# A transformer layer on one core: where the first x is normalized, and who normalizes the first feed-forward rows

## The chip, the cores and the metric

One Trainium2 chip, one of its cores. The metric is the device time of one execution in microseconds. The kernel is written with one block of instructions per engine (TensorE, VectorE, ScalarE, GpSimd and SyncE, which issues all transfers), synchronized by semaphores; each engine works through its own list in order.

## The reference

16 batches of 512 rows of 512 numbers, 16 heads of 32, a feed-forward width of 2048:

```python
emb = silu(sin_emb(timestep)) @ W_ada + b_ada
scale, shift = split(emb, 2)
x = ln(src) * (1 + scale) + shift
q, k, v = x @ Wq + bq, x @ Wk + bk, x @ Wv + bv
scores = q @ k.T / sqrt(32) + attention_bias          # 16 x 16 x 512 x 512 biases, 268 MB
probs = softmax(where(mask, -inf, scores))
x = x + ((probs @ v) @ Wo + bo)
h = ln(x) * g2 + beta2
x = x + (gelu2(h @ W1 + b1) @ W2 + b2)                # gelu2(t) = t * sigmoid(1.702 t)
out = rotations of x's groups of four columns by theta and phi
```

## The kernel before

All large products are made of parts: each float32 operand is split into a high part (rounded by ScalarE) and a low part (operand minus high part, by VectorE or GpSimd), and three matmuls add up to one product.

**The setup block** (`setup_block`) runs first, as a block of its own, and a barrier of all engines ends it. SyncE loads small inputs, W_ada, the first batch's x (`load_x(sp, 0)`) and Wq, Wk, Wv in this order. VectorE makes the angles and silu, TensorE the modulation (`mod`), ScalarE scales Wq and makes the high parts WH of the three weights, VectorE their low parts WL.

**The attention stage** (`attention_stage`) goes over the batches in bodies: START prepares batch 0, then one body for each batch, with 64 slots in each body; x of the next batch is normalized and projected in the slots of the present one. Before slot 0 of START, VectorE takes the statistics of batch 0's x (`moments`, L874, and `aggregate`, L883) and GpSimd makes rstd (`spread_of`, L628 and L630) and the normalized rows (`norm`, L635). TensorE turns x (L716); ScalarE and VectorE modulate it and GpSimd makes its low part (`split_x`, L640). SyncE has in START's order: five bias loads (L546), three small loads and Wo (L574 to L576), the store of the normalized rows (`normal_rows`, L595, waits for `normed`), the load of the next x (L282, waits for that store and for the turning), the mask, and copies of q's and k's rows into the stacked form that the scores need (`stack_rows`, L560). VectorE's statistics of the next x stand among its low parts of q and k.

**The feed-forward stage** (`ffn_stage`) takes the batches in pairs p, each of q = p. For the first pair everything ahead of the eight pair steps is written out at the start of the stage: `project` (L1409) multiplies the context of row tile j by Wo, `modulate` (GpSimd, L1636) and `add` (VectorE, L1735 to L1744) make the residual row y and its mean and variance, `power` (GpSimd) makes rstd (L1645) and adds the second bias b2 (L1655), VectorE's `normalize` (L1751) makes z in place, `turn` (TensorE, L1421) turns z, `take_columns` and `split_columns` (ScalarE L1509 and L1520, VectorE L1789) make the parts of h. The row tiles are j = 0 to 7, four for each batch e of the pair. Then come eight steps s: seven products of the first layer (L1368, a Strassen-like scheme over the two batches), the gelu, and the second layer's matmuls onto ps_out (L1388). In the first pair only, each step also makes the parts of W1 for the step after it (`make_sums` on GpSimd, L1616 to L1621; `make_w1` on ScalarE L1494 and VectorE L1727) and of W2 (`make_w2`, ScalarE L1499, GpSimd L1625), stores them to DRAM for the later pairs, and in steps 4 to 7 GpSimd modulates the first batch's and second batch's rows of the next pair. In every step GpSimd makes two low parts of the gelu's output (`split_g`, L1607). SyncE's order in these steps is written out in `first`.

GpSimd's list in a step of the first pair is: make_sums(s + 1), modulations if any, split_g(2s), make_w2(2s), split_g(2s + 1), make_w2(2s + 1). TensorE takes the results in the step after.

## Time and profile before

| | us |
|---|---|
| three timed runs | 3285.91, 3292.41, 3293.02 (median 3292.41) |
| the profiled execution, its own time | 3286.79 |
| its span, first to last instruction | 3285.0 |
| TensorE busy | 3159.6 (96%) |
| VectorE, ScalarE, GpSimd busy | 2141.5, 1859.9, 2015.2 |
| mean granted TensorE clock | 0.993 |
| attention stage | about 34 to 1660 us of the span |
| feed-forward stage | about 1662 us to the end |

The profile is of one execution. The timeline shows each instruction with its start in microseconds of the span, its length, and in brackets how long its engine had idled before it and what ended that. The busy share of an engine says little of one stage; the waits in a stage do.

### The profile page before, as it was taken

How to read it: one execution, taken by the hardware profiler on the slowest of the kernel's cores; microseconds unless marked ns; L12 is line 12 of the kernel's file. 1: busy time of each engine (PE TensorE's matmuls, PEld its weight loads, DVE VectorE, ACT ScalarE, POOL GpSimd, SP SyncE). 2: the span in 40 equal slices, each digit the busy share in tenths (PEclk: the TensorE clock that was granted, in tenths of full speed). 3: DMA queues.
4: the chain of work that ended last, by engine and by line, in shares of the span. 5: the costliest groups of instructions: out<-in, count | busy, mean ns of one | idle time of the engine just before them, and what ended most of it. 6: DMA issues, size and time to landing. Idle time of an engine off the chain costs nothing. (4 is left out here: it accounts for less than half of the span.)

```text
span 3285.0 us, 52375 instructions
## 1 busy us (share of the span) xinstructions
PE 3159.6 (96%) x16592; PEld 2373.3 (72%) x16592; DVE 2141.5 (65%) x4445; ACT 1859.9 (57%) x4041; POOL 2015.2 (61%) x1247
## 2 busy tenths in 40 slices
PE   5999999999999999999969999999999999999998
PEld 4777777777777777767638688787877868687787
DVE  3777778777777777877757654554645555464542
ACT  2777777777777777777725243342434434253443
POOL 3888888888878888878745633435333443434413
PEclk9999999999999999999989999999999999999999
DMA  5999999998999999998857677675767757586665
GB/s 188 263 267 272 261 274 279 263 265 270 261 271 267 268 261 264 275 270 261 259 157 269 211 246 222 188 254 180 256 205 221 243 185 247 181 261 207 200 204 166
DMA packets 440432, 785.15 MB, mean 239 GB/s; under 512 B 57024, under 2 KB 106176, under 8 KB 440160
## 3 DMA queue, kind: packets, MB, share of 16 engines
q1 hardware_dynamic: 440160, 781.82, 79.3%
q8 instruction: 135, 2.21, 0.3%
q14 instruction: 137, 1.12, 0.1%
HBM read 591.76 MB, written 89.19 MB: 207 GB/s over the span
## 5 line engine op out<-in xcount | busy, mean ns | idle before, releaser
L671 POOL TENSOR_TENSOR biasm<-biasm,maskb 128x1024 f32<-128x1024 f32 x512 | 1091.8, 2152 | 241.6 <-DMA biasm<-in_fside_Bx16xSxS_dram 238.4
L1388 PE MATMUL ps_out<-w_ring,g_hi 128*128 128x512 f32 x2048 | 678.7, 398 | 15.9 <-POOL w_ring L1625 7.9
L1368 PE MATMUL ps_first<-h_hi,w_ring 128*128 128x512 f32 x1792 | 553.4, 390 | 7.5 <-issue 7.4
L1607 POOL TENSOR_TENSOR g_lo<-g_now,g_hi 128x512 fp32r<-128x512 f32 x128 | 169.3, 1323 | 618.1 <-ACT g_hi L1485 618.1
L776 PE MATMUL ps_score<-k_rows,q_rows 96*128 96x512 f32 x1024 | 493.1, 482 | 3.7 <-issue 3.3
L1388 PEld LDWEIGHTS ps_out<-w_ring,g_hi 128*128 128x128 f32 x2048 | 385.6, 188 | 110.4 <-issue 30.8
L827 ACT ACTIVATE probT<-ps_probT 128x512 f32<-128x512 f32 x512 | 305.2, 596 | 239.6 <-PE ps_probT L789 162.2
L917 DVE CUSTOM_DVE_ANT_0 prob_first<-ps_score,biasm 128x512 f32<-128x512 f32 x512 | 346.9, 684 | 142.7 <-PE ps_score L776 104.0
L917 DVE CUSTOM_DVE_ANT_0 prob_last<-ps_score,biasm 128x512 f32<-128x512 f32 x512 | 346.5, 686 | 139.1 <-PE ps_score L776 109.6
L789 PE MATMUL ps_probT<-ident,prob_first 128*128 128x128 f32 x2048 | 392.9, 273 | 16.8 <-DVE probT L496 10.4
L1388 PE MATMUL ps_out<-w_ring,g_lo 128*128 128x512 f32 x1024 | 399.7, 390 | 0.0
L1368 PEld LDWEIGHTS ps_first<-h_hi,w_ring 128*128 128x128 f32 x1792 | 337.0, 188 | 78.5 <-issue 8.8
L853 ACT ACTIVATE prob_last<-prob_last,negmax 128x512 f32<-128x512 f32 x512 | 366.2, 717 | 47.3 <-DVE negmax L917 45.5
L853 ACT ACTIVATE prob_first<-prob_first,negmax 128x512 f32<-128x512 f32 x512 | 365.0, 716 | 47.1 <-DVE negmax L917 46.3
L789 PE MATMUL ps_probT<-ident,prob_last 128*128 128x128 f32 x2048 | 390.5, 272 | 0.0
L789 PEld LDWEIGHTS ps_probT<-ident,prob_first 128*128 128x128 f32 x2048 | 280.9, 140 | 143.8 <-DVE probT L496 20.4
L496 DVE COPY probT<-ps_probT 128x512 f32<-128x512 f32 x512 | 346.9, 678 | 41.2 <-PE ps_probT L789 38.1
L1368 PE MATMUL ps_first<-h_lo,w_ring 128*128 128x512 f32 x896 | 349.2, 390 | 0.0
L1472 ACT ACTIVATE tmp<-tmp 128x512 f32<-128x512 f32 x256 | 162.2, 634 | 248.3 <-DVE tmp L1835 150.0
L1607 POOL TENSOR_TENSOR g_lo<-g_later,g_hi 128x512 fp32r<-128x512 f32 x128 | 174.1, 1360 | 179.0 <-ACT g_hi L1485 178.9
L776 PEld LDWEIGHTS ps_score<-k_rows,q_rows 96*128 96x128 f32 x1024 | 194.3, 190 | 111.5 <-DVE negmax L917 93.7
L1485 ACT ACTIVATE g_hi<-g_later 128x512 fp32r<-128x512 f32 x128 | 80.6, 630 | 332.4 <-PE ps_out L1388 288.2
(159 smaller groups left out, 5606.8 us busy)
## 6 DMA issues: line engine op xcount, KB each, us to landing
biasm<-in_fside_Bx16xSxS_dram SPq DMA_DIRECT2D x512, 512.0 KB, 7.2
w_ring<-w_parts SPq DMA_DIRECT2D x240, 512.0 KB, 3.7
w_ring<-w_parts SPq DMA_DIRECT2D x392, 256.0 KB, 3.5
k_rows<-k_hi SPq DMA_DIRECT2D x512, 64.0 KB, 6.0
q_rows<-q_hi SPq DMA_DIRECT2D x512, 64.0 KB, 4.0
xn<-in_x_dram SPq DMA_DIRECT2D x16, 1024.0 KB, 8.0
normal_rows<-xn SPq DMA_DIRECT2D x16, 1024.0 KB, 9.2
k_rows<-k_lo SPq DMA_DIRECT2D x256, 64.0 KB, 5.6
```

Source lines behind the costliest of these rows:

```text
L496: copy(probT[:, j % GH, i, :], ps_probT[:, place["p", NT * j + i] % 2, :]).then_inc(done.sem, 1)
L671: pool.tensor_tensor(tile, tile, maskb[:, 2 * half:2 * half + 2, :], ALU.add).then_inc(masked.sem, 1)
L776: pe.matmul(ps_score[:, (TL * sb_ + n) % NS, :], stacked[0][sg % 2][:, sj % GH, si * P:(si + 1) * P], stacked[1][sg % 2][:, sj % GH, :], s ...
L789: mm = pe.transpose(ps_probT[:, k % 2, tq * P:(tq + 1) * P], probs(b, j, tq)[:, i * P:(i + 1) * P], ident[:, :])
L827: copy_out(act, 0, outT_act, lambda o, ps: act.activation(o, ps, ACT.Copy), mode, b, j, i)
L853: e = act.activation(probs(tb, tj, ti), probs(tb, tj, ti), ACT.Exp, bias=negmax[:, tj % 2, ti:ti + 1], scale=-1.0, accum_out=sums[:, (tj / ...
L917: dve.tensor_tensor_reduce(probs(tb, tj, ti), ps_score[:, (TL * tb + n) % NS, :], biasm[:, bias_place(tb, n // 2)[0], n % 2, :], -1.0, LOW ...
L1368: mm = pe.matmul(ps[:, BANK[n], :], w1r[:, place, w, cols], h[:, n, c, :], start=(c == 0 and k == 0 and not onto), stop=(c == 1 and k == 2 ...
L1388: mm = pe.matmul(ps_out[:, t, :], a[:, k % 2, cols], w2r[:, k % VR, w, :], start=(m == 0 and n == 0), stop=(m == NF - 1 and n == 2))
L1472: act.activation(tmp[:, I_TH[i % 2], :], tmp[:, at, :], ACT.Tanh, scale=SIGMOID_RATE / 2).then_inc(th_done.sem, 1)
L1485: act.activation(GHI[:, k % 2, :], src, ACT.Copy).then_inc(ghi_done.sem, 1)
L1607: pool.tensor_tensor(GLO[:, k % 2, :], src, GHI[:, k % 2, :].bitcast(F32), ALU.subtract).then_inc(glo_done.sem, 1)
```

## The change

**In the setup block** the order of the three weights becomes Wk, Wq, Wv, in SyncE's loads and in ScalarE's high parts. VectorE takes batch 0's statistics there, before any low part, and normalizes x between the low parts of Wk and Wq. GpSimd makes rstd and the low part of Wv. The same work is gone from START. **In the feed-forward stage's first pair** ScalarE normalizes the rows: a short instruction makes shift = -mean * rstd and a full one z = y * rstd + shift, into the last eight places of g_later, so that y stays in y_rows. VectorE only makes -mean (`less_mean`). GpSimd's b2 adds leave `power` and become `add_b2`, four in step 0 (into y_sum) and four in step 1 (in place, in y_rows). TensorE turns the first batch after projecting row tile 5. SyncE's order changes with it: the rows of mod behind the first context, b2 behind the second batch's contexts, the stores of y in step 2, the loads for the next pair in steps 1, 3 and 4, and W1's last four raw pairs wait for the second turning. GpSimd's modulations for the next pair are in steps 3, 4, 6 and 7.

```diff
-                for n in range(3):
+                for n in (1, 0, 2):
...
+                eps_added.wait(pool, -1, 0)
+                pool.tensor_tensor(rstd[:, :], var_eps[:, :], half_pow[:, :], ALU.pow).then_inc(pow_done.sem, 1)
+                pool.wait_ge(scaled, 1 + NC * 3)
+                for c in range(NC):
+                    pool.tensor_tensor(WL[2][:, c, :], wst[:, 2, c, :], WH[2][:, c, :].bitcast(F32), ALU.subtract)
...
-                for n in range(3):
-                    dve.wait_ge(scaled, 1 + NC * (n + 1))
+                x_in.wait(dve, -1, 0)
+                for t in range(NC):
+                    dve.bn_stats(stats[:, t, :], xn[:, t, :]).then_inc(stats_made.sem, 1)
+                stats_made.wait(dve, -1, NC - 1)
+                for t in range(NC):
+                    dve.bn_aggr(mean_var[:, t, :], stats[:, t, :]).then_inc(stats_done.sem, 1)
+                stats_done.wait(dve, -1, NC - 1)
+                dve.tensor_scalar(var_eps[:, :], mean_var[:, :, 1], EPS, None, ALU.add).then_inc(eps_added.sem, 1)
+                for n in (1, 0):
+                    dve.wait_ge(scaled, (1 + 2 * NC, NC)[n])
                     for c in range(NC):
                         dve.tensor_tensor(WL[n][:, c, :], wst[:, n, c, :], WH[n][:, c, :].bitcast(F32), ALU.subtract)
+                    if n == 1:
+                        pow_done.wait(dve, -1, 0)
+                        dve.sem_inc(dve_waited, 1)
+                        for t in range(NC):
+                            dve.tensor_scalar(xn[:, t, :], xn[:, t, :], mean_var[:, t, 0:1], rstd[:, t:t + 1],
+                                              ALU.subtract, ALU.mult).then_inc(normed.sem, 1)
...
-                act.wait_ge(w_in[0], 16)
-                act.mul(wst[:, 0, :, :], wst[:, 0, :, :], QSCALE).then_inc(scaled, 1)
-                act.wait_ge(scaled, 1)
-                for n in range(3):
+                for n in (1, 0, 2):
                     act.wait_ge(w_in[n], 16)
+                    if n == 0:
+                        act.mul(wst[:, 0, :, :], wst[:, 0, :, :], QSCALE).then_inc(scaled, 1)
+                        act.wait_ge(scaled, NC + 1)
...
-                    spread_of(-1)
-                    for t in range(NT):
-                        norm(-1, t)
                     for c in range(NC):
...
-                    for t in range(NT):
-                        moments(-1, t)
-                    aggregate(-1)
...
+    def place_of(q, j):
+        return j % 2 if q else j
+    def z_of(q, j):
+        return yr[:, j // NT, j % NT, :] if q else g1[:, NF - 2 * NT + j, :]
...
+                if q == 1:
+                    y2_done.wait(sp, 0, NT * e + NT - 1)
+                if (q, e) == (1, 1):
+                    for s in range(2):
+                        sp.wait_ge(y_out[s], y_out_at(0, 2 * NT - 2 + s))
                 sp.dma_start(yr[:, e, :, :], normal_dram[2 * q + e, :, :].rearrange("(t p) d -> p t d", p=P))\
...
+                        zT_done.wait(sp, 0, 2 * NC - 1)
                     for blk in range(2):
                         f = s + blk * NS
...
+                sp.dma_start(wo[:, :, :], Wo.rearrange("(c p) d -> p c d", p=P)).then_inc(wo_in, 16)
+                load_ctx(0, 0, 0)
                 load_rows(0, 0)
-                sp.dma_start(wo[:, :, :], Wo.rearrange("(c p) d -> p c d", p=P)).then_inc(wo_in, 16)
-                for t in range(2):
-                    load_ctx(0, 0, t)
-                sp.dma_start(b2_rows[:, :], b2.unsqueeze(0).broadcast_to([P, D])).then_inc(late_in, 16)
+                load_ctx(0, 0, 1)
                 for tile, src in ((g2_col, g2), (beta2_col, beta2), (b1_col, b1)):
...
                     load_ctx(0, 1, t)
-                for s in range(2):
+                sp.dma_start(b2_rows[:, :], b2.unsqueeze(0).broadcast_to([P, D])).then_inc(late_in, 16)
+                for s in range(3):
                     load_raw(s)
-                for j in range(NT, 2 * NT):
-                    store_y(0, j)
                 for m in range(2):
...
                     load_raw_w2(m)
-                for s in range(2, NS):
+                for s in range(3, NS):
...
                         r = (NS * p + s) * NW + n
                         load_w1(r + WR)
+                        if p == 0 and n == 0 and s == 2:
+                            for j in range(NT, 2 * NT):
+                                store_y(0, j)
...
-                    if s == (0 if p else 2) and ahead:
-                        for e in range(2):
-                            load_normal(p + 1, e)
+                    if s == (0 if p else 3) and ahead:
+                        load_normal(p + 1, 1)
+                    if s == (0 if p else 1) and ahead:
+                        load_normal(p + 1, 0)
                         load_rows(p + 1, 0)
+                    if s == (0 if p else 4) and ahead:
                         for t in range(NT):
                             load_ctx(p + 1, 0, t)
                     if 2 <= s <= NT + 1 and p > 0:
...
-                    if s == (NT if p else NT + 1) and ahead:
+                    if s == NT and ahead:
                         load_rows(p + 1, 1)
...
-            for e in range(2):
-                for i in range(NC):
-                    turn(0, e, i)
+                if j == NT + 1:
+                    for i in range(NC):
+                        turn(0, 0, i)
+            for i in range(NC):
+                turn(0, 1, i)
...
+            def normalize(j):
+                e, t = divmod(j, NT)
+                pow_done.wait(act, 0, j)
+                act.activation(shift[:, j:j + 1], less_mean[:, j:j + 1], ACT.Copy, scale=rstd[:, j:j + 1]).then_inc(shift_made, 1)
+                act.wait_ge(shift_made, j + 1)
+                act.activation(z_of(0, j), yr[:, e, t, :], ACT.Identity, bias=shift[:, j:j + 1], scale=rstd[:, j:j + 1])\
+                    .then_inc(z_done.sem, 1)
+            for j in range(NT + 1):
+                normalize(j)
+            for i in range(NC):
+                take_columns(0, 0, i)
+            for k in range(4):
+                split_columns(0, k)
+            normalize(NT + 1)
+            normalize(NT + 2)
+            make_w1(0, range(NW))
+            normalize(NT + 3)
+            for i in range(NC):
+                take_columns(0, 1, i)
+            split_columns(0, 4)
+            split_columns(0, 5)
...
             def power(q, j):
+                k = place_of(q, j)
+                var_done.wait(pool, q, j)
+                pool.tensor_tensor(rstd[:, k:k + 1], var_eps[:, k:k + 1], half_pow[:, 0:1], ALU.pow)\
+                    .then_inc(pow_done.sem, 1)
+                if q > 0:
+                    add_b2(q, j)
+            def add_b2(q, j):
                 e, t = divmod(j, NT)
-                var_done.wait(pool, q, j)
-                pool.tensor_tensor(rstd[:, j % 2:j % 2 + 1], var_eps[:, j % 2:j % 2 + 1], half_pow[:, 0:1], ALU.pow)\
-                    .then_inc(pow_done.sem, 1)
-                if q == 0 and j == 0:
-                    pool.wait_ge(late_in, 16 * 4)
-                if (q, e) == (0, 0):
-                    to = ysum[:, t, :]
+                if q == 0:
+                    if j == 0:
+                        pool.wait_ge(late_in, 16 * 4)
+                    z_done.wait(pool, q, j)
+                    to = yr[:, e, t, :] if e else ysum[:, t, :]
                 else:
                     to = y2[:, j % 2, :]
-                    if (q, e, t // 2) != (0, 1, 0):
-                        pool.wait_ge(y_out[j % 2], y_out_at(q, j) - 16)
+                    pool.wait_ge(y_out[j % 2], y_out_at(q, j) - 16)
                 pool.tensor_tensor(to, yr[:, e, t, :], b2_rows[:, :], ALU.add).then_inc(y2_done.sem, 1)
...
-                        if s == 0:
-                            for i in range(2):
-                                pool.wait_ge(y_out[i], y_out_at(0, 2 * NT - 2 + i))
                         make_sums(s + 1)
-                    at = (2, 3, 6, 7) if p else (4, 5, 6, 7)
+                    at = (2, 3, 6, 7) if p else (3, 4, 6, 7)
                     if ahead and s in at:
                         for j in range(2):
                             modulate(p + 1, 2 * at.index(s) + j)
                     split_g(p, 0, 2 * s)
                     if p == 0:
                         make_w2(2 * s)
+                        if s < 2:
+                            for t in range(NT):
+                                add_b2(0, NT * s + t)
...
-            add(0, 0)
-            for j in range(1, 2 * NT):
+            for j in range(2 * NT):
                 add(0, j)
-                normalize(0, j - 1)
-                if j == 2 * NT - 1:
-                    for k in range(4):
-                        split_columns(0, k)
-            normalize(0, 2 * NT - 1)
+                if j >= 2 * NT - 2:
+                    for k in range(2):
+                        split_columns(0, 2 * (j - 2 * NT + 2) + k)
```

VectorE's list in the setup block, from silu to the block's end, before and then with the change:

```order
L211 TENSOR_SCALAR silu<-silu 128x128
L217 TENSOR_TENSOR wq_lo<-wst,wq_hi 128x512 x4
L217 TENSOR_TENSOR wk_lo<-wst,wk_hi 128x512 x4
L217 TENSOR_TENSOR wv_lo<-wst,wv_hi 128x512 x4
L220 TENSOR_TENSOR mod<-ps_setup,bada 128x128
```

```order
L217 TENSOR_SCALAR silu<-silu 128x128
L223 BN_STATS stats<-xn 128x6 x4
L226 BN_AGGR mean_var<-stats 128x2 x4
L228 TENSOR_SCALAR var_eps<-mean_var 128x4
L232 TENSOR_TENSOR wk_lo<-wst,wk_hi 128x512 x4
L237 TENSOR_SCALAR xn<-xn,mean_var,rstd 128x512 x4
L232 TENSOR_TENSOR wq_lo<-wst,wq_hi 128x512 x4
L241 TENSOR_TENSOR mod<-ps_setup,bada 128x128
```

Statistics and normalization of x came in, and the four low parts of Wv went to GpSimd.

GpSimd's list with the change, at steps 0 and 1 of the first pair (y_b is here the room of W1's sums; g_lo is split_g, w_ring is make_w2):

```order
L1675 TENSOR_TENSOR y_b<-g_later,y_b 128x256
L1661 TENSOR_TENSOR g_lo<-g_now,g_hi 128x512
L1679 TENSOR_TENSOR w_ring<-turned_out,w_ring 128x512
L1715 TENSOR_TENSOR y_sum<-y_rows,b_rows 128x512 x4
L1661 TENSOR_TENSOR g_lo<-g_now,g_hi 128x512
L1679 TENSOR_TENSOR w_ring<-turned_out,w_ring 128x512
L1670 TENSOR_TENSOR y_b<-g_later 128x256
```

The row with x4 is new; before, the second g_lo followed directly on the first w_ring.

ScalarE's list with the change, from the end of the first batch's splits at the start of the stage:

```order
L1558 ACTIVATE h_hi<-tmp 128x512 x4
L1577 ACTIVATE shift<-less_mean,rstd 128x1
L1579 ACTIVATE g_later<-y_rows,shift,rstd 128x512
L1577 ACTIVATE shift<-less_mean,rstd 128x1
L1579 ACTIVATE g_later<-y_rows,shift,rstd 128x512
L1532 ACTIVATE w_ring<-g_later 128x256
```

The shift and g_later rows are new; five such pairs stand at the start of ScalarE's list, these two are row tiles 5 and 6, and tile 7 follows on the seven w_ring instructions.

## Rows read from the trace of the kernel before

**Rows 1.** Timeline, 10 to 52 us: SyncE, ScalarE, VectorE, TensorE, GpSimd (start, us, what)

```profile
13.49 0.51 SPq L152 DMA_DIRECT2D wst<-in_L_cond_Wk_dram  x1
...
20.73 1.91 ACT L236 ACTIVATE wst<-wst 128x2048 f32<-128x2048 f32 x1 [6.35 <-DMA wst<-in_L_cond_Wq_dram]
...
26.85 2.17 ACT L241 ACTIVATE wv_hi<-wst 128x512 fp32r<-128x512 f32 x4
...
29.72 2.49 DVE L217 TENSOR_TENSOR wv_lo<-wst,wv_hi 128x512 fp32r<-128x512 f32 x4
...
34.01 1.86 PE L744 MATMUL ps_probT<-ident,mod 128*16 128x128 f32 x8 [4.92 <-PEq L133]
46.55 1.97 PE L716 MATMUL ps_fill<-ident,xn 128*128 128x128 f32 x8 [10.68 <-POOL xn L635]
...
38.24 8.26 POOL L635 TENSOR_SCALAR xn<-xn,mean_var,rstd 128x512 f32<-128x512 f32 x4
```

**Rows 2.** DMA issues, 0 to 75 us: count, KB each, median us to landing

```profile
wst<-in_L_cond_Wk_dram SPq DMA_DIRECT2D x1, 1024.0 KB, 9.9
...
normal_rows<-xn SPq DMA_DIRECT2D x1, 1024.0 KB, 4.3
...
q_rows<-q_lo SPq DMA_DIRECT2D x4, 64.0 KB, 2.0
```

**Rows 3.** Timeline, 46 to 71 us: SyncE's queue, then TensorE

```profile
46.52 0.37 SPq L595 DMA_DIRECT2D normal_rows<-xn  x1
...
58.94 0.60 SPq L560 DMA_DIRECT2D k_rows<-k_hi  x1
...
68.39 0.59 SPq L560 DMA_DIRECT2D q_rows<-q_lo  x1
...
70.52 0.71 PE L776 MATMUL ps_score<-k_rows,q_rows 96*128 96x512 f32 x1 [3.32 <-issue]
```

**Rows 4.** Timeline, 1660 to 1716 us: TensorE, GpSimd, VectorE

```profile
1672.07 17.05 PE L1409 MATMUL ps_first<-wo,ctx 128*128 128x512 f32 x32 [13.45 <-DMA ctx<-context_t]
1689.69 14.00 PE L1409 MATMUL ps_out<-wo,tmp 128*128 128x512 f32 x32 [0.57 <-DMA tmp<-context_t]
1703.53 1.91 PE L1421 MATMUL ps_first<-ident,y_rows 128*128 128x128 f32 x16
1712.97 3.33 PE L1421 MATMUL ps_first<-ident,y_rows 128*128 128x128 f32 x16 [7.52 <-DVE y_rows L1751]
...
1704.34 1.27 POOL L1655 TENSOR_TENSOR y_b<-y_rows,b_rows 128x512 f32<-128x512 f32 x1
...
1706.60 0.69 DVE L1738 TENSOR_TENSOR y_rows<-ps_out,y_rows 128x512 f32<-128x512 f32 x1
...
1712.38 0.54 DVE L1751 TENSOR_SCALAR y_rows<-y_rows,mean_var,rstd 128x512 f32<-128x512 f32 x1
```

**Rows 5.** TensorE's waits and the chain, 1790 to 1850 us; windows with clock, DMA share, GB/s

```profile
PE ps_out L1388 <- POOL w_ring L1625: 7.9, 3, 5.7
...
1836.80 5.44 PE ps_out L1388 x12
1842.24 2.73 PE ps_first L1368 x12
...
1836.80:1842.24 5.44, 5.44 (x13) 4.29 (x14) 2.15 (x3) 0.00 (x0) 5.36 (x5) 0.51 0.83 262
```

**Rows 6.** Timeline, 1740 to 1829 us: GpSimd, then TensorE

```profile
1740.01 1.39 POOL L1607 TENSOR_TENSOR g_lo<-g_now,g_hi 128x512 fp32r<-128x512 f32 x1 [3.70 <-ACT g_hi L1485]
1741.36 1.28 POOL L1625 TENSOR_TENSOR w_ring<-turned_out,w_ring 128x512 fp32r<-128x512 f32 x1
...
1795.72 1.75 POOL L1607 TENSOR_TENSOR g_lo<-g_now,g_hi 128x512 fp32r<-128x512 f32 x1
...
1827.49 1.30 POOL L1636 TENSOR_TENSOR y_rows<-y_rows,mod_now_rows 128x512 f32<-128x512 f32 x1 [4.32 <-DMA mod_now_rows<-mod_rows]
...
1743.90 0.39 PE L1388 MATMUL ps_out<-w_ring,g_hi 128*128 128x512 f32 x1
```

51 lines of the change are left out of this document (25 added, 26 removed).

## The prediction

> **What bounds the kernel now.** I read the page first: its chain of waits names almost only TensorE's lines, and TensorE's row of slices is at 9 tenths but for the first slice and the slice at half of the span. So time can be won only where TensorE stands still, and the change touches three such places. I then read the timeline of all engines from 18 to 52 us, the list of DMA issues of the first 75 us, SyncE's queue there, the timeline from 1660 to 1720 us, and the chain and TensorE's waits from 1790 to 1850 us.
>
> *Place A, the start.* The setup block keeps ScalarE and VectorE busy with the high and low parts of the weights [rows 1]: ScalarE scales Wq for 1.91 us, then makes three groups of four high parts (the last of 2.17 us) to 29.0 us, VectorE the low parts to 32.2 us (and five short ones to 32.8). Only after that block do the statistics of x run, and then GpSimd normalizes x for 8.26 us (38.24 to 46.50) while TensorE waits: its transposes of x start at 46.55 us with 10.68 us idle ahead of them, a normal TensorE start being possible right behind its eight small transposes of 34.01 us.
>
> *Place B, the start of the feed-forward stage.* TensorE waits for the first context until 1672.07 us, projects the first batch for 17.05 us, waits 0.57 us more, projects the second from 1689.69 us and turns the first batch at 1703.53 us. Then it idles 7.52 us until VectorE has normalized the last row tile (0.54 us at 1712.38) and turns the second batch at 1712.97 us [rows 4]. GpSimd's bias add of 1.27 us per tile stands in the same chain.
>
> *Place C, the eight pair steps of the first pair.* TensorE is ahead of GpSimd in three of them: 7.9 us in three waits, the longest 5.7 us, all for GpSimd's low parts of W2 [rows 5]. In the longest, GpSimd itself waited 4.32 us for the rows mod_now_rows [rows 6]. Behind it the granted clock was 0.51, the lower of TensorE's two levels (1.2 GHz), and twelve matmuls took 5.44 us; the next twelve took 2.73 us [rows 5]. So these steps lose 7.9 + 2.7 = 10.6 us.
>
> **The change part by part.**
>
> *A.* VectorE takes the statistics while it would wait for weights. x is ahead of the weights in SyncE's queue and the first weight is there at 20.7 us, when ScalarE stops waiting for it [rows 1], so x is too. Four statistics, each no longer than the 0.69 us of an add [rows 4], and under 2 us of short ones end by 25.5, which is where the low part of Wk ends as well (Wk now lands first, at 20.7: high part to 22.9, low part 2.5 us more). The normalization on VectorE, four tensor_scalar of 0.54 us [rows 4], costs 2.2 us. ScalarE now waits for Wq, second in the queue, until 13.49 + 9.9 = 23.4 us [rows 1, 2]: scale to 25.3, high parts to 27.5, those of Wv to 29.7 us. GpSimd makes the low part of Wv behind all twelve: four tensor_tensor; with the 1.27 us of its 128x512 add [rows 4] it ends at 29.7 + 5.1 = 34.8 us. That is 2.0 us behind the old end, so the next block starts 2.0 us later: TensorE at 36.0, its transposes of x at 36.0 + 1.5 = 37.5 us instead of 46.55. At most **9.0 us** are won.
>
> What is late next is the queue of transfers. SyncE issues 2.5 MB of bias and 1 MB of Wo from 36 us on, and the store of the normalized rows now right behind them. 1 MB takes 2.7 us in this queue (Wq there at 20.7, Wk at 23.4), so 3.5 MB and the store take at least 12.2 us from about 38 us, and more at the rate that the store alone shows, 4.3 us for 1 MB. The store lands between 50.3 and 53 us, against 46.52 + 4.3 = 50.8 before [rows 2, 3]; SyncE waits for it before it loads the next x and only then issues the row copies. Their first went out at 58.94 us, the one that released the first scores at 68.39 + 2.0, and TensorE scored at 70.52 us [rows 3]: 11.6 us from first copy to score. With the first copy at 52 to 53.5 us instead of 58.94 the gain is 5.4 to 7 us. I take **6.0 us**, nearest to this chain; the ends are 9.0 us (queue no limit) and 1 us (x and the copies held until the next x has landed, 5 us behind the store).
>
> *B.* The rows of mod (512 KB) go behind the first context and b2 (256 KB) behind the second. By the 4.3 us per MB of [rows 2] the first projection starts 1.9 us earlier and the second batch's context is there 1.1 us earlier: 1688.6 us. Then TensorE needs 1703.53 - 1689.69 = 13.8 us for its four tiles and now also 1.9 us for the turning of the first batch in between: 1704.3 us. Behind the last tile come VectorE's add (0.69), statistics (about as long) and three short ones, GpSimd's power, and ScalarE's shift and scaling; I take 3.5 us together, five times the add, and 1.0 us because VectorE does two splits of h before that tile [rows 4]: the second turning starts at 1708.8 instead of 1712.97, **4.2 us** won. ScalarE has eight pairs of instructions more, a full one of about 0.54 us (a quarter of the 2.17 in [rows 1]) and a short one each; it idled until the first turning, so five are hidden and the other three fall into waits for TensorE. Ends: 5.5 us (no split in the way), 2 us (the contexts land as before, and ScalarE's queue adds 1 us).
>
> *C.* The rows of mod for the second half come one step earlier, as do the loads and modulations of the first half (steps 3, 4, 6, 7 instead of 4 to 7). The 5.7 us wait and the slow twelve matmuls go (8.4 us), the two others (7.9 - 5.7 = 2.2 us) stay, two steps earlier at most, and step 6 gets one like them, about 1.0 us: 3.2 us for modulations. What is new are four bias adds in each of steps 0 and 1. GpSimd idles 3.70 us there, and TensorE needs the low part of W2 1743.90 - (1741.36 + 1.28) = 1.26 us after it is done [rows 6]. Four adds of 1.27 are 5.1 us, 1.4 more than the idle time. Beside VectorE's gelu GpSimd's subtraction took 1.75 instead of 1.39 us [rows 6], so four of the six instructions at 0.4 us longer make 1.5 us. Step 0: 2.9 - 1.26 = 1.6 us of stall. Step 1 has no slack left: 2.9 us, and 0.5 us since VectorE's own subtractions slide behind. Together **5.0 us**. After: 8.2 us instead of 10.6, **2.4 us** won. Ends: 7.4 us won (adds free) and 5 us lost (twice the lock, and the slow clock twice).
>
> The lock has a rule. The Trainium skill (SBUF — State Buffer, Who interferes with whom) says that a VectorE instruction with two SBUF inputs and a GpSimd one that reads SBUF exclude each other for their whole length. The trace agrees in kind: GpSimd's 1.39 us became 1.75. By that rule in full GpSimd would wait out two gelus and four subtractions in each step, about 1.2 us more per step, and C would win nothing: 3279 us, inside the forecast's own range below.
>
> *Sum.* 6.0 + 4.2 + 2.4 = 12.6 us. Everything behind runs as before, since TensorE is the bound there and only starts sooner. The profiled execution took 3286.8 us (span 3285.0), so 3274.2. The three timed runs are 3285.91, 3292.41 and 3293.02, median 3292.41. The profiled one lies 5.6 us below the median, at the lower end of the four times; I start from their middle, about 3290, and say **3277 us**. A measurement of this kernel tells about 0.2% (6.6 us) from no change.
>
> **The rivals.**
>
> *The adds are hidden.* GpSimd's idle time and slack in steps 0 and 1 are 3.7 + 1.26 us against 5.1: nearly even without the lock. Then C wins 7.4 us and the whole is 17.6: 3272 us. Against it: VectorE's long gelus in each modulated step. Chance 0.2.
>
> *The queue eats place A.* If the store lands at 53 us or later and VectorE's statistics of the next x, ahead of its low part of q, hold the copies until that x is there, A wins 1 to 2 us: total about 8.5, 3281.5 us. For it: SyncE waits for one transfer after the other there; against: copies took 9.45 us of issue, which hides part of the wait. Chance 0.18.
>
> *Slower: GpSimd becomes the bound of every step.* In steps 0, 1, 3, 4 and 6 sums, splits, and four adds or modulations hold it beyond TensorE's step, and each time TensorE idles as long as it did once: 5.7 + 2.7 = 8.4 us, five times that is 42 against the old 10.6, so 31 lost and 10.2 won at A and B: 3311 us. It decides where the waits grow from 1 to 3 us each to those near 5.7 us, behind which the clock was low. Against it: the two other modulated steps stalled 2.2 us together. Chance 0.05.
>
> *The normalization isn't hidden.* If x lands late, VectorE's queue holds all low parts and A loses 2 us, with B and C as forecast: 4.6 us won, 3285 us, no change. The queue order speaks against it. Chance 0.05.
>
> **How the numbers follow.** My forecast has 0.52: 3277, its own range 3270 to 3284 by the ends of B and C. Faster by over 0.2%: nearly all of it, all of the first rival and most of the second, 0.83; within 0.2%: the fourth and the rests, 0.12; slower 0.05. The range reaches from the first rival with A at its best (3265) to the second with a slow median (3287).
>
> **What would show it.** Right: no GpSimd normalization before TensorE's first transposes of x, these near 37.5 us, the first score near 64.5; the second turning near 4 us closer behind the start of the stage; no wait of GpSimd for mod_now_rows and no stall over 4 us in the eight steps, but stalls of 1.5 to 3 us behind the adds of steps 0 and 1. Wrong: the first score later than 68 us, the second turning not closer than before, or twelve matmuls at 5.4 us inside the steps.

## The result

| | before | changed |
|---|---|---|
| runs, us | 3279.1 to 3293.0 (5) | 3251.6 to 3260.1 (5) |
| median, us | 3285.91 | 3258.87 |
| profiled execution, us (span) | 3286.8 (3285.0) | 3258.8 (3256.8) |
| ratio of the runs | | 0.9914, 95% interval 0.9899 to 0.9929 |

The changed kernel is about 28 us faster (0.86% of 3286; interval 23 to 33). The forecast was 3277 us, 12.6 us of gain by its sum; the direction was right, and the time lies below the range (3265 to 3287).

### The profile page after: what moved, and what is told of

It reads as the page before. It is cut to its first block and busy times, and to the rows that moved or that the text cites. A ratio compares the mean times of both kernels' runs of the same rounds, so it can differ in the third digit from the quotient of the medians.

```text
span 3256.8 us, 52383 instructions
## 1 busy us (share of the span) xinstructions
PE 3149.3 (97%) x16592; PEld 2372.1 (73%) x16592; DVE 2148.9 (66%) x4446; ACT 1867.5 (57%) x4057; POOL 2015.7 (62%) x1246
## 5 line engine op out<-in xcount | busy, mean ns | idle before, releaser
L691 POOL TENSOR_TENSOR biasm<-biasm,maskb 128x1024 f32<-128x1024 f32 x512 | 1091.1, 2151 | 227.0 <-DMA biasm<-in_fside_Bx16xSxS_dram 224.9
```

Source lines behind the costliest of these rows:

```text
L691: pool.tensor_tensor(tile, tile, maskb[:, 2 * half:2 * half + 2, :], ALU.add).then_inc(masked.sem, 1)
```

## The profile after

The start (timeline of the changed kernel, 18 to 38 us; start, us, engine, line, op, out<-in, count, idle before and what ended it), against [rows 1]:

```profile
18.15 2.47 DVE L223 BATCH_NORM_STATS2 stats<-xn 128x6 f32<-128x512 f32 x4 [3.27 <-DMA xn<-in_x_dram]
...
23.24 1.91 ACT L259 ACTIVATE wst<-wst 128x2048 f32<-128x2048 f32 x1 [0.40 <-DMA wst<-in_L_cond_Wq_dram]
...
25.29 1.91 DVE L237 TENSOR_SCALAR xn<-xn,mean_var,rstd 128x512 f32<-128x512 f32 x4
...
29.54 5.18 POOL L166 TENSOR_TENSOR wv_lo<-wst,wv_hi 128x512 fp32r<-128x512 f32 x4 [7.18 <-ACT wv_hi L262]
...
35.96 1.87 PE L764 MATMUL ps_probT<-ident,mod 128*16 128x128 f32 x8 [7.12 <-PEq L134]
37.61 1.92 PE L736 MATMUL ps_fill<-ident,xn 128*128 128x128 f32 x8
```

Each of these stands within 0.2 us of where the forecast put it: Wq at 23.4, the end of GpSimd's low parts at 34.8 (29.54 + 5.18 = 34.7), TensorE at 36.0, its transposes of x at 37.5 instead of 46.55. Further on, 40 to 67 us, against [rows 3]:

```profile
40.86 1.47 SPq L618 DMA_DIRECT2D normal_rows<-xn  x1
52.43 0.37 SPq L303 DMA_DIRECT2D xn<-in_x_dram  x1
52.85 0.60 SPq L583 DMA_DIRECT2D k_rows<-k_hi  x1
...
59.03 0.69 DVE L894 BATCH_NORM_STATS2 stats<-xn 128x6 f32<-128x512 f32 x1 [9.46 <-DMA xn<-in_x_dram]
59.64 0.73 DVE L960 SCALAR_TENSOR_TENSOR q_lo<-ps_fill,bqk,q_hi 128x512 fp32r<-128x512 f32 x1
...
66.45 0.40 PE L796 MATMUL ps_score<-k_rows,q_rows 96*128 96x512 f32 x1
```

SyncE stands from 42.3 to 52.4 us on the store of the normalized rows, then loads the next x and only then copies rows; VectorE waits 9.46 us for that x with q_lo queued behind it. The first score is at 66.45 instead of 70.52 us: 4.1 of the 6.0 us.

The start of the feed-forward stage, against [rows 4]:

```profile
1649.75 16.51 PE L1445 MATMUL ps_first<-wo,ctx 128*128 128x512 f32 x32 [10.92 <-DMA ctx<-context_t]
...
1667.95 7.13 PE L1445 MATMUL ps_out<-wo,tmp 128*128 128x512 f32 x16 [1.69 <-DMA tmp<-context_t]
1674.92 1.91 PE L1457 MATMUL ps_first<-ident,g_later 128*128 128x128 f32 x16
...
1688.22 3.01 PE L1457 MATMUL ps_first<-ident,g_later 128*128 128x128 f32 x16 [4.51 <-ACT g_later L1579]
```

From the first projection to the second turning it is 38.5 us instead of 40.9. But the first projection itself starts 22.3 us earlier, where A and B together had 7.9 us to give by then (6.0 and 1.9). The first pair's steps 0 and 1, against [rows 5, 6]: TensorE's waits in 1690 to 1850 us (us in total, times, longest), then GpSimd's timeline.

```profile
PE ps_out L1424 <- POOL w_ring L1679: 7.8, 5, 2.3
```

```profile
1707.74 1.30 POOL L1661 TENSOR_TENSOR g_lo<-g_now,g_hi 128x512 fp32r<-128x512 f32 x1 [15.16 <-ACT g_hi L1523]
1709.00 1.80 POOL L1679 TENSOR_TENSOR w_ring<-turned_out,w_ring 128x512 fp32r<-128x512 f32 x1
1710.75 6.31 POOL L1715 TENSOR_TENSOR y_sum<-y_rows,b_rows 128x512 f32<-128x512 f32 x4
1717.02 1.45 POOL L1661 TENSOR_TENSOR g_lo<-g_now,g_hi 128x512 fp32r<-128x512 f32 x1
1718.43 1.45 POOL L1679 TENSOR_TENSOR w_ring<-turned_out,w_ring 128x512 fp32r<-128x512 f32 x1
...
1725.39 1.30 POOL L1661 TENSOR_TENSOR g_lo<-g_now,g_hi 128x512 fp32r<-128x512 f32 x1 [2.22 <-ACT g_hi L1523]
```

The wait for mod_now_rows is gone, and the longest stall is 2.3 us instead of 5.7. What a step costs is read from TensorE: from the first matmul onto ps_out of one step to that of the next it makes 66 matmuls (a window counts one or two more, those that straddle its ends). Step 1 before, step 0 changed (windows: length in us, busy time and count of PE, PEld, DVE, ACT, POOL, then the granted clock, the transfers' share of 16 engines, GB/s):

```profile
1753.42:1768.38 14.96, 14.96 (x67) 12.39 (x66) 10.12 (x18) 8.32 (x19) 8.39 (x8) 1.00 0.65 229
```

```profile
1712.16:1729.76 17.60, 15.34 (x68) 12.23 (x67) 15.08 (x17) 7.94 (x18) 15.30 (x13) 1.00 0.55 195
```

Steps 0 and 1 took 15.10 and 14.96 us before and take 17.60 and 17.60 us now. GpSimd's first splits of two steps show this badly: they were 14.40 us apart before, less than TensorE's 14.96.

**Where the 28.2 us of span arose.** I cut both profiled executions at the same four events (in us):

| | before | changed | won |
|---|---|---|---|
| to the first score | 70.5 | 66.4 | 4.1 |
| first to last score of the attention stage | 1577.4 | 1561.7 | **15.7** |
| last score to the second turning | 65.1 | 60.1 | 5.0 |
| second turning to the end | 1572.0 | 1568.6 | 3.4 |

More than half lies where no instruction was moved: behind the first score the attention stage has the same instructions in the same order. Two windows of 100 to 1600 us, before and changed:

```profile
100.00:1600.00 1500.00, 1474.14 (x9443) 1081.82 (x9442) 1173.97 (x2894) 1150.18 (x2718) 1269.30 (x646) 1.00 0.94 267
```

```profile
100.00:1600.00 1500.00, 1480.64 (x9535) 1092.91 (x9534) 1186.76 (x2923) 1163.39 (x2751) 1278.30 (x651) 1.00 0.89 270
```

In the same 1500 us TensorE makes 9535 instead of 9443 matmuls (1.0%, which is 15 us) at a clock of 1.00 both times, while the transfers' engines are busy 0.89 instead of 0.94 of the time and still move more. The page says it too, before and changed:

```profile
biasm<-in_fside_Bx16xSxS_dram SPq DMA_DIRECT2D x512, 512.0 KB, 7.2
```

```profile
biasm<-in_fside_Bx16xSxS_dram SPq DMA_DIRECT2D x512, 512.0 KB, 6.0
```

A bias tile lands 6.0 instead of 7.2 us after its issue (median of 512). The trace's single packets of 2048 bytes, counted over 5% to 45% of the execution, take 106 instead of 114 ns in the mean, while the fastest tenth takes 84 ns both times. The engines' own instructions didn't get faster: in the two windows one of VectorE's takes 0.406 us both times in the mean, one of ScalarE's 0.423, GpSimd's addition of the mask to a bias tile 2.15.

What the diff does there that no order of instructions shows: the four small tiles stats, mean_var, var_eps and rstd are now allocated ahead of the setup block. They take 192 bytes of each partition of the on-chip memory (SBUF), so all later tiles of the stage lie 192 bytes further on: in the built programs biasm (the bias tiles) is at byte 200448 instead of 200256, a multiple of 256 instead of 64 past one. Theory one, **addresses**: the transfers run faster so. Theory two, **phase**: the stage's queue only meets in another order because it starts earlier.

## The experiments

Each kernel was timed in turn with the kernel before on the same chip. Five groups ran (e1 to e4, e5 to e8, e9 to e12, e13 to e16, e17 and e18), the second and the last on one chip; in them before had medians of 3285.0, 3278.8, 3287.9, 3278.1 and 3282.0 us, so across groups only ratios are compared, and a gain over before in us is worked out from the ratio. "Stage" is the time from first to last score in the profiled execution.

### Addresses or order

**e1_addresses** (before, only this):

```
-    stats = sb("stats", ...)    # and mean_var, var_eps, rstd, behind rsumT
+    stats = sb("stats", ...)    # the same four, ahead of setup_block(...)
```

> The kernel before with one edit: the four small tiles stats, mean_var, var_eps and rstd are allocated ahead of the setup block, as the change does, and nothing uses them there. So every tile of the attention stage behind mask_raw lies 192 bytes further in SBUF (biasm at 200448 instead of 200256: a multiple of 256 instead of 64 past one), and no instruction moves. Address theory (the attention stage's transfers write and read faster when their tiles lie at multiples of 256 bytes): 12 to 18 us faster than before, mean time of a 2048-byte packet near 106 ns instead of 114. Phase theory (the stage's batches become shorter because the first one starts earlier and its transfers meet in another order): the same as before within 3 us, packets at 114 ns.

Measured: ratio 0.9947 (0.9928 to 0.9966), **17.4 us faster** (11 to 24); stage 1557.9 us, packets 107 ns. The edit moves no instruction, so the phase theory is out: it allowed 3 us.

**e2_old_addresses** (changed kernel, the reverse):

```
+        stats = sb("stats_first", ...)   # four tiles inside the setup block's own memory
-    stats = sb("stats", ...)             # ahead of setup_block
+    stats = sb("stats", ...)             # behind rsumT again
```

> The changed kernel with one edit: the setup block has statistics tiles of its own (inside its own memory) and the stage's four small tiles lie again behind rsumT, so all tiles of the attention stage stand at the addresses of the kernel before, while the order of work is the changed one. Address theory: 12 to 18 us slower than the changed kernel, 9 to 14 us faster than before. Phase theory: within 3 us of the changed kernel.

Measured: 0.9967 (0.9955 to 0.9980), 10.8 us faster than before (7 to 15); stage 1572.2, packets 112 ns. Addresses alone 17.4 and everything else alone 10.8 make 28.2, the measured gain; with intervals of 6 and 4 us either way, so close a match is luck. The order of work is worth 10.8, where the forecast said 12.6.

**e3_ffn_alone** (before up to the end of the attention stage, the changed feed-forward stage behind it):

> The kernel before with the feed-forward part of the change alone: the setup block and the attention stage, addresses included, are those of before. By the record's own sum (4.2 at the start of the feed-forward stage and 2.4 in the first pair's steps) it is 6.6 us faster than before. Read from the two traces it should be about 5 (2.4 to 3.3 at the start, 2.5 in the steps). If the attention stage gains only from what changed in it, its length from the first score to the last context store is that of before.

Measured: 0.9971 (0.9958 to 0.9984), 9.5 us faster (5 to 14). In the profile: last score to second turning 60.4 us instead of 65.1, from there to the end 1569.6 instead of 1572.0; together 7.1. The stage took 1583.9 us with the code and the addresses of before, so one execution's stage varies by some 6 us.

**e4_bias_addresses** (before, the four tiles just ahead of biasm: only biasm and what lies behind it move):

> The kernel before with the four small tiles allocated just ahead of biasm: only biasm, maskb and what lies behind them move by 192 bytes, biasm to a multiple of 256; the q, k and projection tiles and their row copies stay 64 past one. Address theory with all the gain from the bias tiles (three quarters of the stage's bytes): as the run with all tiles moved. With half of it from the row copies: half of that gain, 6 to 9 us. Phase theory: the same as before within 3 us.

Measured: 0.9966 (0.9954 to 0.9979), 11.2 us faster (7 to 15). So moving the bias tiles and what lies behind them brings about two thirds of the 17.4; whether the tiles of the row copies make the rest (6 us, with intervals that overlap) is not settled. The row copies land sooner already with the bias tiles moved: in the window of 100 to 1600 us ScalarE waits 22.7 us for copies of q's rows to make room for q_hi, against 32.2 us before and 17.2 us in the changed kernel. Which of the shortened waits reaches TensorE in the end, that of GpSimd for bias tiles or this one, no run separates.

### Which addresses

**e7_128_past** and **e16_192_past** (before; var_eps and rstd, and for the second negmax and bv_col too, ahead of the setup block: all tiles move by 64 and by 128 bytes), **e10_64_past** (changed kernel; negmax and bv_col ahead too: another 64 bytes, biasm at 200512):

> The kernel before with only var_eps and rstd allocated ahead of the setup block: all tiles of the attention stage behind mask_raw move by 64 bytes, biasm from 64 to 128 past a multiple of 256 (200320). If what counts is a start at a multiple of 256: the time of before within 4 us, packets at 112 to 115 ns. If a multiple of 128 is enough: 12 to 18 us faster, packets near 106 ns. If any shift does it: faster too.

> The kernel before with four small tiles (var_eps, rstd, negmax, bv_col) allocated ahead of the setup block: the attention stage's tiles 128 bytes further, biasm at 200384, 192 past a multiple of 256. If only a start at a multiple of 256 helps: within 4 us of before. If the gain grows with the distance moved (128 past had 4 us): 8 to 12 us faster. If a multiple of 128 had helped a little by itself: slower than e7_128_past, as before.

> The changed kernel with two more small tiles (negmax, bv_col) ahead of the setup block, which moves every tile of the attention stage behind mask_raw by another 64 bytes: biasm at 200512, which is 64 past a multiple of 256 as in the kernel before, though at another address. If the remainder to 256 is what counts: 12 to 18 us slower than the changed kernel again, packets of 2048 bytes 6 to 8% longer. If what counts is something else of the addresses (their order, their distance, a multiple of 64 as such): the changed kernel's time within 3 us.

The changed kernel ran beside e10 as a control:

> The changed kernel itself, for comparison with the other three on the same chip: ratio to before 0.990 to 0.993, packets near 105 ns, DMA share near 0.89 in the stretch 100 to 1600.

| biasm, past a multiple of 256 | ratio to before | packets of 2048 bytes |
|---|---|---|
| 64 (e10) | 0.9944 (0.9932 to 0.9957) | 113 ns |
| 0 (e12, the changed kernel beside it) | 0.9912 (0.9897 to 0.9927) | 106 ns |
| 128 (e7, code of before) | 0.9988 (0.9978 to 0.9998) | 109 ns |
| 192 (e16, code of before) | 0.9999 (0.9986 to 1.0011) | 111 ns |
| 0 (e1, code of before) | 0.9947 (0.9928 to 0.9966) | 107 ns |

e10 and the control, windows as above:

```profile
100.00:1600.00 1500.00, 1473.82 (x9451) 1083.09 (x9451) 1174.07 (x2894) 1154.68 (x2723) 1267.66 (x646) 1.00 0.94 267
```

```profile
100.00:1600.00 1500.00, 1479.61 (x9517) 1091.79 (x9519) 1185.74 (x2920) 1161.27 (x2748) 1276.68 (x651) 1.00 0.89 270
```

64 past is slow again at an address that no other kernel had: 10 us of time (12 to 18 were expected), and the share back at 0.94. 192 past gives nothing that can be measured (0, between 5 faster and 4 slower), 128 past 4 us (0.7 to 7), 0 past 17. The Trainium skill (DMA: Bandwidth & Descriptors, How a descriptor splits into AXI transactions) has a rule for it: a transaction has to start at a multiple of 256 bytes, so a descriptor that doesn't start there begins with one from the multiple below it. Worked out from that for 2048 bytes, an estimate: 9 transactions instead of 8 wherever the start is off. The times agree with it as to 64, 192 and 0; that 128 should be no better than 64, as the rule has it, is just outside e7's interval. And the rule is not the whole account, since the fastest tenth of the packets takes 84 ns at every start. The profiled executions of e7 and e16 had short stages (1560.8 and 1562.6) and shares of 0.92 and 0.93, and made 9537 and 9531 matmuls in 100 to 1600 us, as many as the changed kernel. But the kernel before is faster on their chips (3278.8 and 3278.1 us), and there kernels at 0 past made 9564 to 9593 (e5, e6, e8) and 9564 and 9585 (e13, e14). A profile is one execution of each; the twelve timed runs decide.

**e5_all_aligned** and **e6_ffn_aligned** (changed kernel; small tiles allocated first in both stages, or in the feed-forward stage alone, so that all large tiles start at a multiple of 256):

> The changed kernel with small tiles allocated first in both stages (224 bytes of them), so that every large tile of the attention stage (xn, mask_raw and the weight tiles too, now 64 and 32 past a multiple of 256) and every large tile of the feed-forward stage (now 32 past one) starts at a multiple of 256 bytes. No instruction moves. Address theory: the load of x and the copies of the rows get shorter, and the feed-forward stage's transfers too; TensorE is the bound there (idle 15.9 us before the second layer's products), so 1 to 6 us faster than the changed kernel, 3253 to 3258. Rival (only the bias tiles and row copies, which the change moved already, were held by transfers): the changed kernel's time within 3 us.

> The changed kernel with 224 bytes of small tiles allocated first in the feed-forward stage alone: all its large tiles at multiples of 256 instead of 32 past one. Address theory: its packets get shorter as in the attention stage (about 7%), but TensorE is the bound of the stage, so 0 to 3 us faster than the changed kernel; the DMA share of the stretch 1900 to 3200 falls from some 0.65 to some 0.6.

Measured: 0.9921 (0.9908 to 0.9934) and 0.9924 (0.9911 to 0.9938), which can't be told from the changed kernel's 0.9914. Nor did the share of the transfers fall to 0.6, as expected for e6. 1900 to 3200 us of the changed kernel on the same chip (the run e18 below), of e8 (next section; same chip and same group, tiles not moved) and of e6:

```profile
1900.00:3200.00 1300.00, 1292.77 (x5435) 1003.09 (x5435) 690.40 (x1036) 498.09 (x886) 491.34 (x402) 1.00 0.68 217
```

```profile
1900.00:3200.00 1300.00, 1292.77 (x5435) 1002.98 (x5435) 690.56 (x1036) 498.57 (x886) 492.09 (x402) 1.00 0.66 217
```

```profile
1900.00:3200.00 1300.00, 1292.74 (x5434) 1002.82 (x5434) 689.87 (x1035) 499.12 (x887) 493.47 (x403) 1.00 0.66 217
```

The share goes from 0.68 to 0.66 without the alignment too (e8), and with it e11 has 0.68, so the alignment doesn't set it. It does shorten the packets of 512 bytes in this window: 27.2 or 27.3 ns in the mean in the four kernels with the stage's tiles at multiples of 256 (e5, e6, e11, e14), 28.9 to 29.2 in the other sixteen. Those of 2048 bytes take 98.1 to 99.4 ns with it and 98.6 to 100.2 without. TensorE makes the same matmuls (5434 and 5435): with a third of the transfers' time free, the alignment is worth nothing that I could measure. It paid where the share was 0.94.

### The additions of b2

**e8_adds_spread** (changed kernel):

```
-                        if s < 2:
-                            for t in range(NT):
-                                add_b2(0, NT * s + t)
+                        if s < 4:
+                            for j in range(2 * s, 2 * s + 2):
+                                add_b2(0, j)
...
-                    at = (2, 3, 6, 7) if p else (3, 4, 6, 7)
+                    at = (2, 3, 6, 7) if p else (4, 5, 6, 7)
```

On SyncE the stores of the finished rows (from step 2) and the load of the next pair's second batch (from step 3) go to step 4 with them.

> The changed kernel with GpSimd's eight additions of b2 in twos over the first pair's steps 0 to 3 instead of in fours in steps 0 and 1 (the stores of the finished rows and the load of the next pair's second batch with them, from steps 2 and 3 to step 4, and the modulations from steps 3, 4, 6, 7 to 4, 5, 6, 7). By the record's price of 5.0 us for the additions (stalls behind four in a row), two in a row leave a stall of at most 1 us in each of four steps or none: 2 to 4 us less from the second turning to the end (1568.6 in the changed kernel), 3255 to 3257. Rival (each addition costs its 1.6 us of GpSimd's time wherever it stands, because GpSimd has no slack in these steps): no change.

Measured: 0.9916 (0.9902 to 0.9930), no change; second turning to the end 1568.2 us (1568.6). Step 2 on TensorE, of 66 matmuls as above, then the first matmul onto ps_out of step 4:

```profile
1738.75:1754.20 15.45, 15.25 (x68) 12.31 (x66) 13.75 (x17) 7.95 (x18) 12.38 (x11) 1.00 0.74 273
```

```profile
1772.65 0.47 PE L1424 MATMUL ps_out<-w_ring,g_hi 128*128 128x512 f32 x1 [2.47 <-POOL w_ring L1679]
```

TensorE's stalls of 2.26, 2.27 and 0.98 us are gone from the list. The steps with two additions take 15.42, 15.45 and 15.45 us, against 15.0 to 15.1 without and 17.6 with four; a wait of 0.21 us for VectorE (tmp) is what is left in each. So spread additions do cost less, 1.3 us in three steps where two steps with four lose 5.1. But the next step, which has the last two additions and then the modulations ahead of its low parts, takes 18.45 us, with the stall of 2.47 us above, and the twelve matmuls behind that stall took 4.3 us instead of 2.7 at a granted clock of 0.64. From step 0's first matmul onto ps_out to the next pair's first projection it is 109.9 us instead of 111.3: 1.5 us won, too little to be told from nothing in the timed runs (their interval is 9 us wide). The rival was right that nothing changes, but not in its reason, a fixed price of 1.6 us for each addition.

### The setup part, and what held the first score

**e9_x_last** (changed kernel; in the first pass alone, SyncE's load of the next x last, and VectorE's statistics of it last):

```
-                    if slot == LOAD_AT and b + 2 < B:
+                    if slot == (H * NT - 1 if mode == START else LOAD_AT) and b + 2 < B:
...
-                        if slot in STATS_AT:
+                        if slot in STATS_AT and mode != START:
+                        if mode == START and slot == H * NT - 1:
+                            for t in range(NT):
+                                moments(b + 1, t)
+                            aggregate(b + 1)
-                        if slot == AGGR_AT:
+                        if slot == AGGR_AT and mode != START:
```

> The changed kernel with, in the first pass of the attention stage alone, the load of the second batch's x issued last by SyncE instead of ahead of the row copies (it waits there for the store of normal_rows to land: issued at 52.43, and the first copy of k's rows behind it at 52.85 though k_lo was there at 49.6), and VectorE's statistics of that batch last too (they held VectorE for 9.46 us, q_lo behind them until 59.64). If this pair of waits is what took 1.6 to 2 us of place A's 6.0: first score at 62.5 to 64.5 instead of 66.4, and 2 to 4 us off the time if the attention stage carries the earlier start through to its end. Rival (the queue's 24 copies of 0.6 us bound the first score, or the bias transfers do): the first score stays within 1 us of 66.4.

Measured: 0.9941 (0.9927 to 0.9955), 9 us *slower* than the changed kernel beside it. The first score came at 61.1 us, sooner than expected, so these two waits did hold it. Then:

```profile
83.06 2.47 DVE L894 BATCH_NORM_STATS2 stats<-xn 128x6 f32<-128x512 f32 x4 [13.53 <-DMA xn<-in_x_dram]
```

```profile
86.83 0.80 PE L796 MATMUL ps_score<-k_rows,q_rows 96*128 96x512 f32 x1 [12.61 <-DVE negmax L934]
```

x was issued at 77.5 us, and everything stood behind VectorE. **e11_both** had this and e6's tiles:

> The changed kernel with the late x load and statistics of the run e9_x_last and the feed-forward tiles at multiples of 256 as in e6_ffn_aligned: the gain of the one (2 to 4 us) and of the other (0 to 2), so 2 to 5 us faster than the changed kernel on the same chip. Rival: neither can be told from the changed kernel.

0.9939 (0.9925 to 0.9953), as e9. **e13_x_mid** puts the load of x behind the mask's, in the middle of the row copies; **e14_x_mid_aligned** is that with all tiles at multiples of 256.

> As e9_x_last (which had its first score 5 to 7 us sooner but then lost it: x, issued at 77.5, landed at 83 and VectorE, GpSimd and TensorE stood for 13.5, 10.3 and 12.6 us), but with the load of the second batch's x right behind the mask's load in the middle of the row copies (near 54); VectorE's statistics stay last in the first pass. If the late load was what ate the gain: first score near 61.5, no wait over 4 us of VectorE for x, 3 to 6 us faster than the changed kernel (ratio to before 0.989 to 0.990). Rival (the earlier first score is lost anyway, since the bias transfers behind it don't come sooner): the changed kernel's ratio, 0.991 to 0.992.

> e13_x_mid with every large tile of both stages at a multiple of 256 as in e5_all_aligned. xn, the mask and the feed-forward tiles get shorter packets; on e5_all_aligned this gave nothing that could be told from the changed kernel. Expected: e13_x_mid's time within 3 us, at best 3 us less.

Measured: 0.9928 (0.9915 to 0.9941) and 0.9916 (0.9901 to 0.9931). No long wait for x is left, but the first score is at 64.6 and 65.4 us, not at 61.5 (which transfer holds it there I did not follow), and neither beats the changed kernel (by ratios alone, since it did not run beside them; for e13 0.989 to 0.990 was expected). No version I tried does.

**e15_setup_alone** (changed setup part, old addresses, old feed-forward stage), and, at the new addresses, **e17_no_setup_part** (all of the change but the setup part) against **e18_changed_third**:

> The changed setup block and the changed first part of the attention stage, with the tiles at the addresses of the kernel before (as in e2_old_addresses), and the feed-forward stage of before. Place A alone: first score at 66.4 instead of 70.5. If the stage carries it through: 3 to 5 us faster than before. If the transfers' queue, which limits the stage, gives it back: the time of before within 2 us.

> The changed kernel without the change's setup part: the setup block and the first pass of before, the four small tiles ahead of it (so all addresses of the attention stage are the changed kernel's), and the changed feed-forward stage. If the attention stage carries place A's earlier first score through: 3 to 5 us slower than e18_changed_third, ratio to before near 0.9925. If it gives it back to the transfers: the same within 2 us.

> The changed kernel itself on the same chip as e17_no_setup_part: ratio to before 0.991 to 0.992, as in the two comparisons so far.

Measured: e15 0.9997 (0.9986 to 1.0008), 1 us faster (between 5 faster and 3 slower). e17 0.9933 (0.9921 to 0.9946), one execution of 10329 us is not in it; e18 0.9930 (0.9909 to 0.9951), medians 3262.1 and 3256.1. One of e18's six executions took 3278.3 us at a mean granted clock of 0.944, where the others had 0.991 to 0.994; it pulls that ratio up and widens its interval. So the setup part brings something between nothing and 6 us at the end; whether its whole 3 to 4 us at the first score arrive there stays open.

## Why the prediction was right and wrong

Profiled executions of the same piece of code, averaged, check its terms:

| term | forecast, us | in the pair | mean over kernels |
|---|---|---|---|
| A, first score | 6.0 | 4.1 | 3.2 (70.1 in 7 kernels, 66.9 in 9) |
| B, last score to second turning | 4.2 | 5.0 | 4.1 (64.6 in 6, 60.5 in 9) |
| C, second turning to end | 2.4 | 3.4 | 2.2 (1572.6 in 6, 1570.4 in 9) |
| attention stage | 0 | **15.7** | 20 (1578.0 in 5 at 64 past, 1558.3 in 8 at 0 past) |

The last mean mixes chips; what the stage is worth is better taken from runs timed on one chip, 17 us (e1) and 10 us (e10 against e12).

*The step that failed* is one sentence of the sum: "Everything behind runs as before, since TensorE is the bound there and only starts sooner". It was wrong on both counts. The stage did not run as before, because 192 bytes of small tiles, which the whole diff shows in plain sight (four lines moved in attention_stage; the extract ahead of the prediction doesn't have them), move its bias tiles and the tiles of its row copies to multiples of 256 (x and the mask's own tile stay where they were). Without a moved instruction that alone won 17.4 us (e1). And TensorE is not the only bound there: its slices stand at 9 tenths, but the page's row of the transfers stood at 9 too, and GpSimd waited 238.4 us for bias tiles, the line that fell to 224.9:

```profile
L671 POOL TENSOR_TENSOR biasm<-biasm,maskb 128x1024 f32<-128x1024 f32 x512 | 1091.8, 2152 | 241.6 <-DMA biasm<-in_fside_Bx16xSxS_dram 238.4
```

```profile
L691 POOL TENSOR_TENSOR biasm<-biasm,maskb 128x1024 f32<-128x1024 f32 x512 | 1091.1, 2151 | 227.0 <-DMA biasm<-in_fside_Bx16xSxS_dram 224.9
```

I read the moved allocations as bookkeeping and looked only for moved instructions. With the addresses held, the change is worth 10.8 us against a sum of 12.6 (e2).

*A* was right up to TensorE's transposes and 2 us too high behind them. The rival "the queue eats place A" named the mechanism: SyncE waits out the store, and VectorE's statistics of the next x stand ahead of q_lo. It came true in part, and e9 shows that these waits cost 5 to 7 us at the first score. But SyncE's first row copy (52.85) was within the 52 to 53.5 us of the forecast; what was missed is the second wait. That 13.6 us from the first copy to the score are more than the 11.6 assumed is VectorE's 9.46 us. That the first score's gain arrives at the end of the kernel was assumed too; timed alone (e15) the setup part is 1 us faster (between 5 faster and 3 slower).

*B*: the first projection starts 21.7 us behind the last score instead of 24.2, 2.5 us won where 1.9 were said (by the 4.3 us per MB that the sum names, 512 KB are 2.15). TensorE's wait behind the last tile is 4.5 us where I added up 4.5 (3.5 and 1.0). Right in mechanism and size. B and C together measured 9.5 us in e3 (5 to 14), where the sum has 6.6.

*C* came out as added up. TensorE's steps 0 and 1 take 2.5 and 2.6 us more than before: 5.1 us for the additions, where the sum has 5.0 (though as 1.6 and 3.4). From step 2's first matmul onto ps_out to the next pair's first projection it is 76.1 us instead of 83.2: 7.1 won, 7.4 said. The remaining 1.4 us of the pair's 3.4 lie ahead of step 0, where the sum has nothing, and are chance: from the second turning to step 0's first matmul onto ps_out the old code took 24.7 to 26.0 us in six kernels, the new one 23.9 to 26.0 in nine. In four of these nine step 1 took 19.0 to 19.2 us instead of 17.6, so the mean of C is below the pair's. The split of the 5.0 was less exact: four additions took 6.3 us beside VectorE's work, 1.58 each, where I had 1.27 and 0.4 more for four of six instructions. Stalls of 1.5 to 3 us behind the additions, none over 4 and no slow twelve matmuls: as written. The rival of the hidden additions is out, and so is the slower one. By the full rule on VectorE and GpSimd C would have won nothing; it won 2.2 us in the mean and 3.4 in the pair, which with these spreads speaks against it without ruling it out.

*Luck*: that 10.8 us came out so near 12.6 is in part chance. Timed alone, A brought 1 us of its 6.0 (e15), B and C 9.5 where 6.6 were said (e3), each within 4 to 5 us.

## What to carry to other kernels

In a diff, look at allocations as well as instructions: any tile put ahead of others moves the targets of their transfers, and with the queue near full (a share of 0.94 here) a start at a multiple of 256 bytes was worth 17 us (e1), where all the reordering was worth 11 (e2). Padding cost nothing but bytes here: put the small tiles where they bring the large ones to such a start. A busy row of 9 tenths for TensorE doesn't make it the only bound; count its matmuls per stretch, and read the row of the transfers beside it.

## What the runs showed of the hardware

- A tile's start in SBUF changes the time of transfers to it: in the attention stage packets of 2048 bytes took 104 to 108 ns in the mean with the tiles at a multiple of 256, 112 to 114 ns at 64 past (two addresses), and the fastest tenth 84 ns everywhere.
- Neither 128 nor 192 past is as fast as 0: 4 and 0 us of 17.
- In the feed-forward stage, where the share of the transfers was 0.66 to 0.69, the alignment shortened packets of 512 bytes (27.2 instead of 29 ns) and gave no time.
- Additions of 128x512 that GpSimd makes beside VectorE's work took 1.58 us each in fours; four of them stretched TensorE's step from 15.0 to 17.6 us, two to 15.45.
- In e8 twelve matmuls behind a stall of 2.47 us took 4.3 us instead of 2.7, at a granted clock of 0.64.
